# Experts of a decoder layer: ScalarE writes the high part of each Gelu result, VectorE only subtracts

## The chip, the cores and the metric

The kernel runs on one core of a Trainium2 chip. The metric is the device time of one execution in microseconds (us), from the first to the last instruction and what little lies around them. The time of the kernel before is the median of three runs. Everything else that is said of it comes from one further execution, which the hardware profiler recorded.

## The reference

One decoder layer in float32: self attention with a residual and a layer norm, cross attention to a context with a residual and a layer norm, and then a layer of eight experts, again with a residual and a layer norm. Only the experts are touched. Each token goes to the one of 8 experts with the highest logit; an expert takes at most 768 of the 4096 tokens (rows of 512 values).

```
buf = jnp.zeros((E, C, D), dtype=x.dtype).at[chosen_e, pos_c].add(x_flat * kept[:, None])
h = jax.nn.gelu(jnp.einsum('ecd,edf->ecf', buf, w1) + b1[:, None, :], approximate=False)
eo = jnp.einsum('ecf,efd->ecd', h, w2) + b2[:, None, :]
y = eo[chosen_e, pos_c] * (chosen_p * kept.astype(x.dtype))[:, None]
```

with E = 8 experts, C = 768 slots, D = 512 and F = 2048 hidden values.

## The kernel before, in words

Three stages follow each other: self attention (lines up to about 700), cross attention (to about 1570) and `experts` (from 1572). Only `experts` is changed. The trace has its first matmul at 2783.6 us.

**What is computed how.** TensorE multiplies in the rounded format fp32r. To keep float32's precision, every operand is held in two parts, a high part (the value rounded to fp32r) and a low part (the value minus its high part), and each product is three matmuls: high x high, high x low, low x high (`PARTS`). So weights, inputs and hidden values all go through two elementwise instructions: a rounding copy, and a subtraction that needs the copy.

**Tiling.** The experts run one after the other. An expert's hidden values are made in 16 steps of 128 values (four quads of four steps; `q` counts quads, `j` steps within one). In step `j` TensorE does `first_layer(j)`, 12 matmuls for each half of the slots into `h_bank[0]` and `h_bank[1]` (a half is 384 slots, `HALF`), and then `second_layer(j - 1)`, three matmuls of 512 columns for each tile of 128 slots, summed in `acc[t]` over the whole expert. How many tiles an expert works on is chosen at run time from its count of tokens (`VARIANTS`: 3, 4, 5 or 6). With 3 tiles the second half has no columns and gets no matmuls, but ScalarE and VectorE still process both halves.

**ScalarE's order in a step** (one loop over all 32 quads, lines 1720 to 1738): the high part of w1 for step `j + 1` (L1717), the high part of w2 for step `j` (L1732, which waits for a `second_layer`), then the Gelu of each half from PSUM into `h` (L1737), each after its half's matmuls. Each quad has two loads of an activation table, one ahead of the first copy (L1717) and one ahead of the first Gelu (L1737).

**VectorE's order in a step** (`quad`, from 1787): the low part of w1 for step `j + 1` (L1763), the low part of w2 (L1792), then for each half the high part of `h` (L1798, wait for `h_ready`) and its low part (L1800, wait for `hT_hi`, which counts L1798), then whatever is due of the work for other experts: in the steps `j = 0` and `j = 1` of quads 1 to 3 `split_x` (L1756, L1758), which takes 128 transposed slots of the next expert's input out of `h_bank[0]` in two instructions; and pieces of the previous expert's residual and norm (L1771, L1774, L1776, L1784).

**Who waits for it.** `second_layer(j)` waits for `hT_ready`, which counts L1800. `first_layer` of the steps 1 and 2 of quads 1 to 3 waits for `x_ready`, which counts L1758 (the transposes of L1839 and the next `first_layer` use the same `h_bank[0]`), so each `split_x` stands between two matmul groups. SyncE loads the next weights when `w1_ready` and `w2_ready` say that L1763 and L1792 are through. GpSimd loads the next expert's rows (L1676) and scatters the previous expert's (L1690).

Of the kernel before, what the change touches and what calls it, by code (L numbers as in the profile page):

```python
# [10 lines left out]
ACT = mybir.ActivationFunctionType  # L11
# [24 lines left out]
def wait_alone(engine, sem, value, waited):  # L36

    engine.wait_ge(sem, value)
    engine.sem_inc(waited, 1)
# [1530 lines left out]
def experts(nc, z, a):  # L1573
# [13 lines left out]
    HALF = CAP // 2  # L1587
# [12 lines left out]
    with ExitStack() as ctx:  # L1600
# [11 lines left out]
        h = s.sb("h", [P, 2, CAP])  # L1612
        hT = s.sb("hT", [P, 2, 2, CAP], F32R)
# [16 lines left out]
        h_mm, h_ready, hT_hi, hT_ready = s.sem("h_mm"), s.sem("h_ready"), s.sem("hT_hi"), s.sem("hT_ready")  # L1630
# [81 lines left out]
        @block.scalar  # L1712
        def _(act):
            def high_w1(hidden, j):

                act.wait_ge(h_mm, hidden + 2 * FREE)
                act.activation(w1[:, j % 2, 0, :, :], w1_in[:, j // 2, :, j % 2 * P:(j % 2 + 1) * P], ACT.Copy).then_inc(w1_hi, 1)  # L1717

            act.wait_ge(b1_ready, 1)
            act.wait_ge(w_in[0], 32)  # L1720
            high_w1(0, 0)
            with act.Fori(0, E * QUADS) as eq:
                n = act.snap(eq * 4)
                n2 = act.snap(eq * 8)
                for j in range(4):

                    if j % 2:
                        act.wait_ge(w_in[(j + 1) // 2 % 2], (eq + 1 + (j + 1) // 4) * 32)
                    high_w1(n2 + 2 * j, (j + 1) % 4)

                    act.wait_ge(o_mm, n + j - 1 + FREE)
                    act.activation(w2[:, j % 2, 0, :], w2_in[:, j // 2, j % 2, :], ACT.Copy).then_inc(w2_hi, 1)  # L1732
                    for half in range(2):
                        act.wait_ge(h_mm, n2 + 2 * j + half + 2 * FREE + 1)

                        act.wait_ge(hT_ready, n2 + 2 * j + half - 3 + 2 * FREE)
                        act.activation(h[:, j % 2, half * HALF:(half + 1) * HALF], h_bank[half][:, 0:HALF], ACT.Gelu,  # L1737
                                       bias=b1[:, bass.ds(n + j, 1)]).then_inc(h_ready, 1)

        @block.vector  # L1740
        def _(dve):

            for t in range(VARIANTS[0], TS):
                dve.memset(acc[t][:, :], 0.0).then_inc(acc0, 1)
            dve.sem_inc(hT_ready, 2 * FREE)
            dve.sem_inc(w1_ready, FREE)
            dve.sem_inc(w2_ready, FREE)
            dve.wait_ge(b1_mm, 1)
            dve.tensor_copy(b1[:, :], acc[0][:, 0:E * STEPS]).then_inc(b1_ready, 1)

            def split_x(e, t, buf, bank):

                cols = slice(t * P, (t + 1) * P)
                src = bank[:, :].rearrange("p (k q) -> p k q", k=KC)
                dve.wait_ge(x_mm, e * TS + t + 1)
                dve.tensor_scalar(xT[:, buf, 0, :, cols], src, 0.0, None, ALU.add).then_inc(x_hi, 1)  # L1756
                dve.wait_ge(x_hi, e * TS + t + 1)
                dve.tensor_tensor(xT[:, buf, 1, :, cols], src, xT[:, buf, 0, :, cols].bitcast(F32), ALU.subtract).then_inc(x_ready, 1)  # L1758

            def low_w1(n, j):  # L1760

                dve.wait_ge(w1_hi, n + 1)
                dve.tensor_tensor(w1[:, j % 2, 1, :, :], w1_in[:, j // 2, :, j % 2 * P:(j % 2 + 1) * P],  # L1763
                                  w1[:, j % 2, 0, :, :].bitcast(F32), ALU.subtract).then_inc(w1_ready, 1)

            def add_rows(e, t):


                dve.wait_ge(in_rows, (e + 1) * 16)
                dve.wait_ge(out_ready, e * TS + t + 1)  # L1770
                dve.scalar_tensor_tensor(out=out[:, t, :], in0=out[:, t, :], scalar=rows[:, t, C:C + 1],  # L1771
                                         in1=rows[:, t, 0:C], op0=ALU.mult, op1=ALU.add).then_inc(sum_ready, 1)
                dve.wait_ge(sum_ready, e * TS + t + 1)
                dve.bn_stats(stat[:, t, :], out[:, t, :]).then_inc(stat_ready, 1)  # L1774
                wait_alone(dve, stat_ready, e * TS + t + 1, waited)
                dve.bn_aggr(mv[:, t, :], stat[:, t, :]).then_inc(mv_ready, 1)  # L1776

            def add_eps(e):
                dve.wait_ge(mv_ready, (e + 1) * TS)
                dve.tensor_scalar(var_eps[:, :], mv[:, :, 1], EPS, None, ALU.add).then_inc(ve_ready, 1)  # L1780

            def scale_rows(e, t):
                dve.wait_ge(rstd_ready, e + 1)
                dve.tensor_scalar(out[:, t, :], out[:, t, :], mv[:, t, 0:1], rstd[:, t:t + 1], ALU.subtract, ALU.mult).then_inc(y_ready, 1)  # L1784

            def quad(e, q):
                par = e % 2
                n, n2 = (e * QUADS + q) * 4, (e * QUADS + q) * 8
                for j in range(4):
                    low_w1(n + j + 1, (j + 1) % 4)  # L1790
                    dve.wait_ge(w2_hi, n + j + 1)
                    dve.tensor_tensor(w2[:, j % 2, 1, :], w2_in[:, j // 2, j % 2, :], w2[:, j % 2, 0, :].bitcast(F32), ALU.subtract).then_inc(w2_ready, 1)  # L1792

                    dve.wait_ge(o_mm, n + j - 1 + FREE)
                    for half in range(2):
                        cols = slice(half * HALF, (half + 1) * HALF)
                        dve.wait_ge(h_ready, n2 + 2 * j + half + 1)
                        dve.tensor_copy(hT[:, j % 2, 0, cols], h[:, j % 2, cols]).then_inc(hT_hi, 1)  # L1798
                        dve.wait_ge(hT_hi, n2 + 2 * j + half + 1)
                        dve.tensor_tensor(hT[:, j % 2, 1, cols], h[:, j % 2, cols], hT[:, j % 2, 0, cols].bitcast(F32), ALU.subtract).then_inc(hT_ready, 1)  # L1800
                    if q > 0 and j < 2:
                        split_x(e + 1, 2 * q - 2 + j, 1 - par, h_bank[0])
                    if e > 0 and (q, j) in ADD_AT:
                        add_rows(e - 1, ADD_AT[q, j])
                    if e > 0 and (q, j) == EPS_AT:
                        add_eps(e - 1)
                    if e > 0 and (q, j) in SCALE_AT:
                        for t in SCALE_AT[q, j]:
                            scale_rows(e - 1, t)

            for t in range(TS):
                split_x(0, t, 0, h_bank[t % 2])
            low_w1(0, 0)
            for e in range(E):
                for q in range(QUADS):
                    quad(e, q)
                dve.wait_ge(in_b2, (e + 1) * 16)

                dve.wait_ge(scattered, e * TS * 16)
                dve.wait_ge(o_mm, (e + 1) * STEPS + FREE)  # L1820
                for t in range(TS):
                    dve.tensor_tensor(out[:, t, :], acc[t][:, :], b2[:, :], ALU.add).then_inc(out_ready, 1)  # L1822
            for t in range(TS):
                add_rows(E - 1, t)
            add_eps(E - 1)
            for t in range(TS):
                scale_rows(E - 1, t)
# [159 lines left out]
```

## Time and profile before

| | |
|---|---|
| median of 3 runs | 3785.6 us (3783.69 to 3785.71) |
| profiled execution | 3778.94 us |
| its span, first to last instruction | 3777.2 us |
| experts stage in the span | from 2783.6 us |
| PE, DVE, ACT, POOL busy over the span | 92%, 67%, 46%, 54% |
| mean granted TensorE clock | 0.955 |

PE is TensorE, DVE VectorE, ACT ScalarE, POOL GpSimd; PEld is TensorE's weight loading. A granted clock of 1.0 is 2.4 GHz, of 0.5 is 1.2 GHz. A group of instructions is named by its line in the kernel. The busy shares are means over three stages with different limits, so they say little on one edit in the last stage; that has to be read from the stage's own steps.

### The profile page before, as it was taken

How to read it: one execution, taken by the hardware profiler on the slowest of the kernel's cores; microseconds unless marked ns; L12 is line 12 of the kernel's file. 1: busy time of each engine (PE TensorE's matmuls, PEld its weight loads, DVE VectorE, ACT ScalarE, POOL GpSimd, SP SyncE). 2: the span in 40 equal slices, each digit the busy share in tenths (PEclk: the TensorE clock that was granted, in tenths of full speed). 3: DMA queues.
4: the chain of work that ended last, by engine and by line, in shares of the span. 5: the costliest groups of instructions: out<-in, count | busy, mean ns of one | idle time of the engine just before them, and what ended most of it. 6: DMA issues, size and time to landing. Idle time of an engine off the chain costs nothing. (4 is left out here: it accounts for less than half of the span.)

```text
span 3777.2 us, 51836 instructions
## 1 busy us (share of the span) xinstructions
PE 3470.1 (92%) x18133; PEld 2274.6 (60%) x18134; DVE 2519.5 (67%) x4522; ACT 1754.4 (46%) x3098; POOL 2045.9 (54%) x1031
## 2 busy tenths in 40 slices
PE   7999999999999999999999858899869889899985
PEld 5455455455454554554544336788758778788874
DVE  6777777777777777777777336788634755466566
ACT  2555555555555555555555533343323433343343
POOL 2789898888988898888898820011110100110112
PEclk9999999999999999999999878999879999999998
DMA  6321322313122223223110032222132422232332
GB/s 219 95 62 55 93 63 66 98 48 97 57 65 85 66 67 91 64 66 99 48 40 12 7 98 74 81 82 77 65 114 71 136 88 97 95 104 100 118 117 99
DMA packets 190735, 309.76 MB, mean 82 GB/s; under 512 B 25609, under 2 KB 72329, under 8 KB 190490
## 3 DMA queue, kind: packets, MB, share of 16 engines
q1 hardware_dynamic: 164330, 238.58, 20.3%
q0 software_dynamic: 15072, 45.89, 3.5%
q10 hardware_dynamic: 11088, 22.02, 1.7%
q8 instruction: 153, 2.51, 0.3%
q14 instruction: 92, 0.75, 0.1%
HBM read 197.23 MB, written 61.33 MB: 68 GB/s over the span
## 5 line engine op out<-in xcount | busy, mean ns | idle before, releaser
L463 DVE TENSOR_REDUCE sa_part_max<-sa_mx 128x1 f32<-128x512 f32 x2048 | 1281.9, 680 | 541.5 <-PE sa_mx L574 537.4
L426 ACT ACTIVATE sa_prob<-sa_sc 128x512 f32<-128x512 f32 x2048 | 1122.0, 595 | 822.5 <-PE sa_sc L620 780.8
L247 POOL TENSOR_TENSOR sa_quad_sum<-sa_quad_sum,sa_prob 128x1024 f32<-128x1024 f32 x512 | 1207.6, 2404 | 7.7 <-ACT sa_prob L426 7.7
L574 PE MATMUL sa_mx<-sa_k_stack,sa_q_stack 96*128 96x512 f32 x2048 | 967.2, 474 | 27.1 <-DVE sa_part_max L463 15.8
L620 PE MATMUL sa_sc<-sa_q_stack,sa_k_stack 98*128 98x512 f32 x2048 | 864.6, 424 | 8.2 <-ACT sa_prob L426 8.2
L247 POOL TENSOR_TENSOR sa_quad_sum<-sa_prob 128x1024 f32<-128x1024 f32 x256 | 616.1, 2429 | 256.1 <-ACT sa_prob L426 256.1
L574 PEld LDWEIGHTS sa_mx<-sa_k_stack,sa_q_stack 96*128 96x128 f32 x2048 | 389.4, 190 | 377.1 <-issue 205.0
L620 PEld LDWEIGHTS sa_sc<-sa_q_stack,sa_k_stack 98*128 98x128 f32 x2048 | 389.1, 190 | 318.8 <-ACT sa_prob L426 273.6
L1856 PE MATMUL ex_h<-ex_xT,ex_w 128*128 128x384 f32 (+2 forms) x2688 | 467.6, 330 | 81.9 <-issue 35.0
L1856 PEld LDWEIGHTS ex_h<-ex_xT,ex_w 128*128 128x128 f32 x2688 | 450.7, 196 | 106.4 <-issue 77.8
L589 PE MATMUL sa_pv<-sa_prob,sa_v 128*32 128x512 f32 x4096 | 501.9, 608 | 0.7 <-ACT sa_prob L426 0.7
L1867 PE MATMUL ex_acc<-ex_w,ex_hT 128*128 128x512 f32 x1728 | 433.3, 397 | 1.4 <-DVE ex_hT L1800 1.4
L1867 PEld LDWEIGHTS ex_acc<-ex_w,ex_hT 128*128 128x128 f32 x1728 | 318.5, 190 | 61.4 <-DVE ex_hT L1800 2.3
L1676 POOL DMA_DIRECT2D ex_xg<-rows x54 | 29.8, 559 | 549.7 <-PE ex_h L1839 549.4
L1798 DVE CAST ex_hT<-ex_h 128x384 fp32r<-128x384 f32 x256 | 92.3, 361 | 272.8 <-ACT ex_h L1737 272.8
L1737 ACT ACTIVATE ex_h<-ex_h,ex_b 128x384 f32<-128x384 f32 x256 | 143.9, 581 | 273.6 <-PE ex_h L1856 273.3
L589 PEld LDWEIGHTS sa_pv<-sa_prob,sa_v 128*32 128x32 f32 x4096 | 108.0, 110 | 245.0 <-issue 241.2
L927 POOL TENSOR_TENSOR ca_rstd<-ca_var_eps,ca_minus_half 128x8 f32<-128x8 f32 x16 | 26.5, 1656 | 393.7 <-DVE ca_var_eps L1010 393.7
L490 DVE RECIPROCAL sa_recip<-sa_dens 128x128 f32<-128x128 f32 x128 | 119.9, 941 | 77.4 <-ACT sa_dens L408 77.4
L1732 ACT ACTIVATE ex_w<-ex_w_in 128x512 fp32r<-128x512 f32 x128 | 80.7, 631 | 185.0 <-PE ex_acc L1867 184.3
L1800 DVE TENSOR_TENSOR ex_hT<-ex_h,ex_hT 128x384 fp32r<-128x384 f32 x256 | 143.0, 558 | 8.9
L1685 POOL TENSOR_TENSOR ex_rstd<-ex_var_eps,ex_minus_half 128x6 f32<-128x6 f32 x8 | 13.9, 1742 | 236.5 <-DVE ex_var_eps L1780 236.5
(201 smaller groups left out, 3397.1 us busy)
## 6 DMA issues: line engine op xcount, KB each, us to landing
ex_w_in<-in_L_ffn_w_dram SPq DMA_DIRECT2D x130, 512.0 KB, 4.3
sa_xT<-xT SPq DMA_DIRECT2D x57, 1024.0 KB, 5.1
sa_q_stack<-sa_hilo SPq DMA_DIRECT2D x372, 64.0 KB, 2.0
sa_k_stack<-sa_hilo SPq DMA_DIRECT2D x360, 64.0 KB, 2.0
ex_xg<-rows POOLq DMA_DIRECT2D x54, 256.0 KB, 3.2
rows<-sa_empty SPq DMA_DIRECT2D x48, 257.0 KB, 3.8
ex_rows<-rows POOLq DMA_DIRECT2D x8, 1542.0 KB, 7.5
sa_prob<-in_x_dram ACTq DMA_DIRECT2D x8, 1024.0 KB, 7.4
```

Of the source, the lines that this page charges most:

```text
L247: pool.tensor_tensor(quad_sum[:, i % 2, heads, :], so_far, prob[:, k, heads, :], ALU.add).then_inc(quad_ready, 1)
L426: act.activation(prob[:, kt % 4, j, :], sc[n % 2][:, :], ACT.Exp, scale=SCALE).then_inc(prob_ready, 1)
L463: dve.reduce_max(part_max[:, q, j, k:k + 1], mx[n % 3][:, :], AX_X).then_inc(max_read, 1)
L490: dve.reciprocal(recip[:, g % 2, cols], dens[:, cols]).then_inc(recip_ready, 1)
L574: pe.matmul(mx[n % 3][:, :], q_stack[0:QK, j, at:at + P], k_stack[0:QK, g // NQ % 2, j, k * BANK:(k + 1) * BANK], start=True, stop=True).t ...
L589: last = pe.matmul(pv[D * j:D * (j + 1), :], v[:, buf, kt, D * j:D * (j + 1)], prob[:, kt % 4, j, :], start=(kt == 0), stop=(kt == T - 1))
L620: pe.matmul(sc[n % 2][:, :], k_stack[0:AUG, g // NQ % 2, j, kt * P:(kt + 1) * P], q_stack[0:AUG, j, g % NQ * BANK:(g % NQ + 1) * BANK], st ...
L1737: act.activation(h[:, j % 2, half * HALF:(half + 1) * HALF], h_bank[half][:, 0:HALF], ACT.Gelu, bias=b1[:, bass.ds(n + j, 1)]).then_inc(h_ ...
L1798: dve.tensor_copy(hT[:, j % 2, 0, cols], h[:, j % 2, cols]).then_inc(hT_hi, 1)
L1800: dve.tensor_tensor(hT[:, j % 2, 1, cols], h[:, j % 2, cols], hT[:, j % 2, 0, cols].bitcast(F32), ALU.subtract).then_inc(hT_ready, 1)
L1856: last = pe.matmul(h_bank[half][:, 0:slots], w1[:, j % 2, pw, k, :], xT[:, buf, px, k, half * HALF:half * HALF + slots], start=(i == 0 and ...
L1867: last = pe.matmul(acc[t][:, :], hT[:, j % 2, ph, t * P:(t + 1) * P], w2[:, j % 2, pw, :], start=(start and i == 0), stop=(stop and i == 2))
```

## The change

The rounding copy of each half of `h` moves from VectorE to ScalarE. ScalarE issues both copies after both Gelus of the step, each behind a wait for its own Gelu. VectorE keeps the subtraction, whose wait for `hT_hi` is now a wait for ScalarE. Tiles, semaphores, counts and the number of instructions in all stay as they are.

```
@@ experts, scalar
                         act.activation(h[:, j % 2, half * HALF:(half + 1) * HALF], h_bank[half][:, 0:HALF], ACT.Gelu,
                                        bias=b1[:, bass.ds(n + j, 1)]).then_inc(h_ready, 1)
+                    for half in range(2):
+                        cols = slice(half * HALF, (half + 1) * HALF)
+                        act.wait_ge(h_ready, n2 + 2 * j + half + 1)
+                        act.activation(hT[:, j % 2, 0, cols], h[:, j % 2, cols], ACT.Copy).then_inc(hT_hi, 1)
@@ experts, vector, quad
                     dve.wait_ge(o_mm, n + j - 1 + FREE)
                     for half in range(2):
                         cols = slice(half * HALF, (half + 1) * HALF)
-                        dve.wait_ge(h_ready, n2 + 2 * j + half + 1)
-                        dve.tensor_copy(hT[:, j % 2, 0, cols], h[:, j % 2, cols]).then_inc(hT_hi, 1)
                         dve.wait_ge(hT_hi, n2 + 2 * j + half + 1)
                         dve.tensor_tensor(hT[:, j % 2, 1, cols], h[:, j % 2, cols], hT[:, j % 2, 0, cols].bitcast(F32), ALU.subtract).then_inc(hT_ready, 1)
```

## Rows read from the trace of the kernel before

**Rows 1.** Busy us by stretch (first line: columns): the stage, a 3-tile expert.

```profile
core 0: us, PE busy (x) PEld busy (x) DVE busy (x) ACT busy (x) POOL busy (x), PEclk, DMA share, GB/s
2784.00:3777.00 993.00, 878.06 (x4608) 785.26 (x4607) 579.58 (x1110) 373.18 (x573) 101.42 (x109) 0.95 0.30 101
...
2926.00:3026.00 100.00, 79.56 (x360) 68.66 (x360) 72.14 (x141) 45.67 (x72) 13.55 (x14) 0.91 0.40 134
```

**Rows 2.** Waits, 2784 to 3777 us: waiter <- releaser: us, times, longest.

```profile
PE ex_h L1856 <- DVE ex_xT L1758: 27.9, 30, 1.8
...
PE ex_acc L1867 <- DVE ex_hT L1800: 1.4, 2, 0.7
```

**Rows 3.** Groups by line and shape: busy us, mean ns | idle before.

```profile
L1737 ACT ACTIVATE ex_h<-ex_h,ex_b 128x384 f32<-128x384 f32 x256 | 143.9, 581 | 273.6 <-PE ex_h L1856 273.3
...
L1798 DVE CAST ex_hT<-ex_h 128x384 fp32r<-128x384 f32 x256 | 92.3, 361 | 272.8 <-ACT ex_h L1737 272.8
...
L1717 ACT ACT_TABLE_LOAD x32 | 41.1, 1283 | 0.6
L1737 ACT ACT_TABLE_LOAD x32 | 41.1, 1283 | 138.1 <-PE ex_h L1856 138.1
...
L1348 ACT ACTIVATE ca_qk<-ca_bank 128x154 fp32r<-128x154 f32 x16 | 4.8, 300 | 1.3 <-PE ca_bank L1540 0.9
...
L1259 ACT ACTIVATE ca_vw<-ca_product 128x512 fp32r<-128x512 f32 x8 | 4.4, 618 | 5.1 <-DMA vw<-ca_x1n 5.1
```

**Rows 4.** Timeline, 4-tile expert, step j = 0 with `split_x`: start, us, engine.

```profile
3449.53 1.06 ACT L1737 ACTIVATE ex_h<-ex_h,ex_b 128x384 f32<-128x384 f32 x2
3450.21 0.36 DVE L1798 CAST ex_hT<-ex_h 128x384 fp32r<-128x384 f32 x1 [2.88 <-ACT ex_h L1737]
...
3450.47 0.63 ACT L1717 ACTIVATE ex_w<-ex_w_in 128x512 fp32r<-128x512 f32 x1
...
3451.47 0.56 DVE L1800 TENSOR_TENSOR ex_hT<-ex_h,ex_hT 128x384 fp32r<-128x384 f32 x1
3451.95 0.68 DVE L1756 TENSOR_SCALAR ex_xT<-ex_h 128x512 fp32r<-128x512 f32 x1
...
3453.59 3.66 PE L1856 MATMUL ex_h<-ex_xT,ex_w 128*128 128x384 f32 x24 [0.99 <-DVE ex_xT L1758]
```

**Rows 5.** Timeline, the same expert, next step (j = 1).

```profile
3457.49 0.58 ACT L1737 ACTIVATE ex_h<-ex_h,ex_b 128x384 f32<-128x384 f32 x1 [0.71 <-PE ex_h L1856]
...
3459.16 0.69 DVE L1756 TENSOR_SCALAR ex_xT<-ex_h 128x512 fp32r<-128x512 f32 x1
```

**Rows 6.** Timeline, 5-tile expert, step j = 1, and the wait before it.

```profile
3332.86 3.78 PE L1856 MATMUL ex_h<-ex_xT,ex_w 128*128 128x384 f32 x24 [0.19 <-DVE ex_xT L1758]
...
3336.88 0.58 ACT L1737 ACTIVATE ex_h<-ex_h,ex_b 128x384 f32<-128x384 f32 x1 [0.85 <-PE ex_h L1856]
...
3338.51 0.69 DVE L1756 TENSOR_SCALAR ex_xT<-ex_h 128x512 fp32r<-128x512 f32 x1
...
3340.38 3.69 PE L1856 MATMUL ex_h<-ex_xT,ex_w 128*128 128x384 f32 x24
```

**Rows 7.** Timeline, 6-tile expert, step j = 1.

```profile
3196.08 0.69 DVE L1758 TENSOR_TENSOR ex_xT<-ex_h,ex_xT 128x512 fp32r<-128x512 f32 x1
...
3197.92 4.35 PE L1856 MATMUL ex_h<-ex_xT,ex_w 128*128 128x384 f32 x24
```

**Rows 8.** Timeline, 3-tile expert, from one quad to the next.

```profile
2944.86 1.05 ACT L1737 ACTIVATE ex_h<-ex_h,ex_b 128x384 f32<-128x384 f32 x2 [1.67 <-PE ex_h L1856]
...
2947.76 0.62 ACT L1732 ACTIVATE ex_w<-ex_w_in 128x512 fp32r<-128x512 f32 x1
...
2949.01 1.28 ACT L1737 ACT_TABLE_LOAD   x1 [0.63 <-PE ex_h L1856]
```

**Rows 9.** Timeline, PE alone, 3-tile expert: after two waits.

```profile
2954.37 4.21 PE L1856 MATMUL ex_h<-ex_xT,ex_w 128*128 128x384 f32 x12 [1.80 <-DVE ex_xT L1758]
...
3002.86 2.34 PE L1856 MATMUL ex_h<-ex_xT,ex_w 128*128 128x384 f32 x12 [1.80 <-DVE ex_xT L1758]
```

More of the change, by code:

```diff
@@ L1738, in _ @@
                                        bias=b1[:, bass.ds(n + j, 1)]).then_inc(h_ready, 1)
+                    for half in range(2):
+                        cols = slice(half * HALF, (half + 1) * HALF)
+                        act.wait_ge(h_ready, n2 + 2 * j + half + 1)
+                        act.activation(hT[:, j % 2, 0, cols], h[:, j % 2, cols], ACT.Copy).then_inc(hT_hi, 1)
         @block.vector
@@ L1796, in quad @@
                         cols = slice(half * HALF, (half + 1) * HALF)
-                        dve.wait_ge(h_ready, n2 + 2 * j + half + 1)
-                        dve.tensor_copy(hT[:, j % 2, 0, cols], h[:, j % 2, cols]).then_inc(hT_hi, 1)
                         dve.wait_ge(hT_hi, n2 + 2 * j + half + 1)
```

## The prediction

> **What bounds the kernel now.** I read the views in this order: busy time by stretch, then who waits for whom, then the timeline around each kind of wait, since the edit touches one stage only. In the experts stage TensorE is busy for 878 of 993 us, VectorE for 580 and ScalarE for 373 [rows 1]: TensorE sets the pace, and neither of the two engines that trade work is full. In a 3-tile expert PE is busy for only 80 of 100 us, and there VectorE is busy for 72 [rows 1]. The eight experts have 6, 3, 5, 6, 5, 4, 4 and 3 tiles (18, 9, 15 ... matmuls of L1867 a step).
>
> The instruction that moves, L1798, costs 256 x 361 ns = 92 us of VectorE [rows 3]. That is no gain by itself: VectorE idles for 272.8 us right before these casts, waiting for the Gelus [rows 3]. What counts is the chain from the Gelus to TensorE. TensorE waits for hidden values (L1800) for only 1.4 us in the whole stage, but for `split_x` (L1758) 30 times, 27.9 us [rows 2]. `split_x` stands in VectorE's queue right behind the second subtraction, so the edit acts through these 30 places. By expert they are: all 12 of the two 3-tile experts, all 12 of the two 4-tile experts, and the 6 with j = 0 in the two 5-tile experts; the 6-tile experts have none. That makes 18 with j = 0 and 12 with j = 1.
>
> **Price of the new instruction.** The trace has no ScalarE copy of 384 columns out of SBUF. Bounds: a copy of 512 columns takes 618 ns, one of 154 takes 300 ns (out of PSUM), and the Gelu of 384 takes 581 ns [rows 3]. The line between the two copies gives 300 + 230 x (618 - 300)/358 = 504 ns at 384 columns. The copies of this stage out of SBUF take 10 ns more than the 618 (L1717, 0.63 us [rows 4]), so I take 0.52 us, near that row, and keep 0.50 and, by the Gelu, 0.58 as ends. ScalarE starts the next instruction before the last has ended: the copy of L1717 starts 0.94 us after the first of two Gelus of 0.58 us each [rows 4], 0.47 us apiece, so an overlap of 0.1 us. A copy of 0.52 then occupies ScalarE for about 0.43 us. VectorE starts 0.10 us after a ScalarE result (Gelu from 3449.53, done after 0.58, cast at 3450.21) [rows 4].
>
> The VectorE cast takes 361 ns against 558 for the subtraction of the same size, so it is the cheaper engine for this copy. The Trainium skill (Perfetto Trace Analysis, Optimizing Scalar/DVE Operations) says that a copy for which VectorE has a fast mode is quicker there, and that moving it to ScalarE may pay where VectorE is saturated. By that rule the change loses; the trace agrees that VectorE is not saturated (580 of 993 us).
>
> The Trainium skill (VectorE: DVE Perf Modes, the section on the TRN2 errata) gives ScalarE's SBUF to SBUF cost as 224 cycles plus one per column at 1.2 GHz. That would be an estimate of 507 ns here and would put the sum below at about 7.4 us; no row shows that size.
>
> **(a) j = 0 steps, and 3-tile steps: both Gelus back to back.** Here the table load holds the Gelus until both halves are ready (or, with 3 tiles, both are ready at once), and they run as a pair. Count from the pair's start. Before: cast at 0.68, second subtraction at 1.94, `split_x` at 2.42 [rows 4]. After: the copies start at 0.95 and 1.38 and end at 1.47 and 1.90; the first subtraction starts at 1.57, the second 0.48 later (the distance from subtraction to next instruction in [rows 4]) at 2.05, `split_x` at 2.53. The cast that VectorE no longer does and the copies that ScalarE does in its place nearly cancel: +0.11 us. All 18 places with j = 0 wait already, so they pay it in full: 18 x 0.11 = 2.0 us. Of the six j = 1 places of the 3-tile experts, two follow a slow stretch of TensorE in which its own transposes (L1839) came last; the other four pay 4 x 0.11 = 0.4 us. The last `second_layer` of a 3-tile expert waits for the last subtraction: 2 x 0.11 = 0.2 us.
>
> **(b) j = 1 steps of 4-tile experts: the Gelus are apart.** Before, the first half's cast and subtraction were done while TensorE was still at the second half. After, both copies sit behind the second Gelu. It starts at 3457.49 [rows 5]; copies at 3457.97 and 3458.40, ending 3458.49 and 3458.92; subtractions at 3458.59 and 3459.07; `split_x` at 3459.55 in place of 3459.16 [rows 5], +0.39 us, all of it on TensorE's wait. 6 x 0.39 = 2.3 us.
>
> **(c) j = 1 steps of 5-tile experts: a new wait.** The second Gelu starts at 3336.88, `split_x` at 3338.51, and TensorE goes on at 3340.38 without waiting [rows 6]. By the same count `split_x` starts at 3338.94, +0.43. `split_x` takes 1.41 us and TensorE starts 0.23 after it (3451.95 to 3453.59 is 1.64) [rows 4], so TensorE starts at 3340.58 at the earliest, 0.20 late, and a group after a wait runs 3.78 us against 3.69 without [rows 6], since its first weights load in the open: 0.28 us in all. 6 x 0.28 = 1.7 us.
>
> **(d) 6-tile experts: nothing.** `split_x` ends at 3196.77, and TensorE takes it up at 3197.92 [rows 7]: 1.15 us of cover against 0.43 of delay. The 16 ordinary steps of any expert don't pay either: `second_layer(j)` starts a whole `first_layer` after the Gelus that it needs, over 3 us with 4 tiles or more, and 4.2 us from the Gelus' start with 3; the second subtraction ends at 2.61.
>
> **(e) What is queued behind the copies on ScalarE.** The copies of L1717 and L1732 and the table loads come 0.85 us later. In experts with 4 to 6 tiles ScalarE has that much idle time ahead of L1732 or the table load of L1737. With 3 tiles it hasn't at a quad's end: L1732 ends at 2948.38, and the table load of L1737 starts at 2949.01, when the matmuls are done [rows 8]. 0.85 later is 2949.23, so the load, the Gelus and `split_x` come 0.23 us later: 3 quads x 2 experts x 0.23 = 1.4 us. If L1732 were held further by a late weight, it would be more. VectorE's subtraction of L1763 starts at 2.53 and finds its high part finished at 2.44, 0.1 us of slack at no cost. SyncE's loads and GpSimd's queue shift by the same tenths and have nobody waiting on them.
>
> **(f) No more table loads.** There are 32 + 32 in 32 quads [rows 3], and L1732 runs behind Gelus in steps 1 to 3 of each quad without one. So a copy right behind a Gelu needs none. The Trainium skill (ScalarE: Activation LUTs, Table sets) has copy in every set; the trace agrees.
>
> Sum: 2.0 + 0.4 + 0.2 + 2.3 + 1.7 + 1.4 = 8.0 us. Against the profiled execution that is 3778.9 + 8.0 = 3786.9 us; the median of the runs is 6.7 us above that execution, so 3793.6 us. A copy of 0.50 us makes the sum about 7; one of 0.58 us (0.48 of occupancy) makes (a) 0.17, (b) 0.45, (c) 0.34 and (e) 0.33 apiece, 11 us in all.
>
> **Rivals.**
> *TensorE's clock.* In the 3-tile experts twelve waits of the same kind are followed by 12 matmuls in about 2.35 us at clock 1.0; after three of them it takes 4.21, 4.20 and 3.02 us, as at 2954.37 [rows 9], with a granted clock near 0.5. The edit makes the idle time before six of them 0.34 us longer. Each further slow group costs 1.86 us; with three to nine more it is 3793.6 + 6 to 17 = 3799 to 3811 us. For it: idle time stands before each fall. Against it: the same 1.80 us stands before a slow and a fast group alike. If instead the three slow groups fall away by the shift of phase, 4.4 us come back: 3789 us.
> *Hidden.* The copies start in Gelus' shadow and some waits end elsewhere (TensorE's transposes): (b) and (c) vanish if `split_x` is held by the transposes. Then +4 us, 3790 us. Against it: the computed starts lie 0.4 us after the transposes end.
> *Faster: VectorE is the late one.* If VectorE is still busy with other work when the pair of Gelus is done, the casts it sheds come off the chain. `split_x` starts 1.74 us after VectorE comes free before, 0.96 after; the edit wins as soon as VectorE comes free later than 0.79 us after the pair's start, and by 0.78 us beyond 1.57. In all 22 places of (a) that is -17 instead of +2.4: 3785.6 - 17 + 2.3 + 1.7 + 1.4 = 3774 us. Against it: the casts there start at 0.68 us, released by the Gelu, after an idle time [rows 4].
> *The edit doesn't do what it says*, for instance a table load per copy: over 3830 us. Point (f) speaks against it.
>
> **How the numbers follow.** Forecast 0.55 (3792 to 3797), more slow groups 0.19, fewer 0.10, hidden 0.11, faster 0.04, table loads 0.01. About 0.2%, 7.6 us here, is what a measurement of this kernel can tell from no change: above 3793.2 is slower, below 3778.0 faster. The forecast lies on that line; I give two thirds of its 0.55 to slower. Slower: 0.36 + 0.19 + 0.01 = 0.56; same: 0.19 + 0.10 + 0.11 = 0.40; faster 0.04. The range goes from the case of fewer slow groups or hidden copies, 3788, to the lower part of the clock case, 3803.
>
> **What the profile after would show.** Copies of 128x384 on ACT at 0.50 to 0.58 us; 64 table loads; in the pair steps `split_x` at 2.53 us from the Gelus' start, not 2.42; 36 waits of PE for L1758 and not 30, some 34 us in place of 27.9; the 6-tile experts unchanged in length. Wrong would be: a copy that waits for its Gelu's end and leaves ScalarE idle, casts' 92 us found again as a shorter stage, or a changed granted clock in the 3-tile experts.

## The result, and the profile after

The changed kernel takes 1.0018 of the time of the kernel before, 95% interval 1.0011 to 1.0025: medians 3791.3 us against 3785.65 us over 20 runs each. By the ratio that is 6.8 us more (4 to 9), where 8.0 were forecast; the two medians alone lie 5.7 us apart. 3791.3 us lies in the range. It is a real loss, since the interval excludes 1, but just under the 0.2% that the prediction took as its line, where it had put 0.56 above and 0.40 within.

The first of these lines, from the page of after, has each engine's busy time; behind it stand two groups (busy us, mean ns | idle before) and four waits of the experts stage (us, times, longest):

```profile
PE 3481.4 (92%) x18133; PEld 2282.3 (60%) x18134; DVE 2416.9 (64%) x4266; ACT 1856.3 (49%) x3354; POOL 2047.5 (54%) x1031
```

```profile
L1742 ACT ACTIVATE ex_hT<-ex_h 128x384 fp32r<-128x384 f32 x256 | 119.1, 517 | 0.0
...
L1737 ACT ACT_TABLE_LOAD x32 | 41.1, 1283 | 128.3 <-PE ex_h L1858 128.2
```

```profile
DVE ex_hT L1802 <- ACT ex_hT L1742: 419.6, 128, 12.8
...
PE ex_h L1858 <- DVE ex_xT L1762: 30.1, 31, 1.9
...
PE ex_h L1841 <- ACT ex_h L1737: 7.3, 6, 1.2
...
PE ex_acc L1869 <- DVE ex_hT L1802: 1.6, 2, 0.8
```

VectorE is 103 us lighter and the kernel is no faster: VectorE now idles 419.6 us ahead of its subtractions, where it idled 272.8 ahead of its casts [rows 3] and 8.9 ahead of its subtractions. ScalarE is 102 us heavier. Its new copy takes 517 ns (0.52 taken), and no table load was added. TensorE's waits for `split_x` (now L1760 and L1762) went from 27.9 to 30.1 us [rows 2].

The timeline of a 4-tile expert of after, first the step j = 0, then j = 1, to be laid beside [rows 4] and [rows 5]:

```profile
3457.28 1.05 ACT L1737 ACTIVATE ex_h<-ex_h,ex_b 128x384 f32<-128x384 f32 x2
...
3458.23 0.94 ACT L1742 ACTIVATE ex_hT<-ex_h 128x384 fp32r<-128x384 f32 x2
...
3458.85 1.03 DVE L1802 TENSOR_TENSOR ex_hT<-ex_h,ex_hT 128x384 fp32r<-128x384 f32 x2 [3.06 <-ACT ex_hT L1742]
...
3459.80 0.68 DVE L1760 TENSOR_SCALAR ex_xT<-ex_h 128x512 fp32r<-128x512 f32 x1
...
3461.44 3.65 PE L1858 MATMUL ex_h<-ex_xT,ex_w 128*128 128x384 f32 x24 [1.08 <-DVE ex_xT L1762]
...
3465.33 0.58 ACT L1737 ACTIVATE ex_h<-ex_h,ex_b 128x384 f32<-128x384 f32 x1 [0.71 <-PE ex_h L1858]
3465.81 0.93 ACT L1742 ACTIVATE ex_hT<-ex_h 128x384 fp32r<-128x384 f32 x2
...
3467.37 0.69 DVE L1760 TENSOR_SCALAR ex_xT<-ex_h 128x512 fp32r<-128x512 f32 x1
...
3469.01 3.63 PE L1858 MATMUL ex_h<-ex_xT,ex_w 128*128 128x384 f32 x24 [0.66 <-DVE ex_xT L1762]
```

In the pair step `split_x` starts 2.52 us after the Gelus (2.42 before), and TensorE's wait is 1.08 us (0.99 before). With the Gelus apart (j = 1) it starts 2.04 after the second Gelu (1.67 before), and the TensorE group behind it, at 3469.01, waits 0.66 us. In the kernel before it waited 0.29:

```profile
3460.81 3.64 PE L1856 MATMUL ex_h<-ex_xT,ex_w 128*128 128x384 f32 x24 [0.29 <-DVE ex_xT L1758]
```

In the 5-tile expert, step j = 1, the distance is 2.04 (1.63 in [rows 6]), and TensorE's weight loads, which followed each other before, now pause for 0.42 us:

```profile
3342.46 0.58 ACT L1737 ACTIVATE ex_h<-ex_h,ex_b 128x384 f32<-128x384 f32 x1 [0.85 <-PE ex_h L1858]
...
3344.50 0.68 DVE L1760 TENSOR_SCALAR ex_xT<-ex_h 128x512 fp32r<-128x512 f32 x1
...
3346.11 0.99 PEld L1858 LDWEIGHTS ex_h<-ex_xT,ex_w 128*128 128x128 f32 x6 [0.42 <-issue]
```

And the 3-tile expert at a quad's start, to be laid beside [rows 8]: the table load follows L1732 without a gap, and the transposes of L1841 wait 1.23 us for the first Gelu. The last row is the same wait in the kernel before (its L1839), 1.02 us.

```profile
2953.18 0.61 ACT L1732 ACTIVATE ex_w<-ex_w_in 128x512 fp32r<-128x512 f32 x1
...
2953.81 1.28 ACT L1737 ACT_TABLE_LOAD   x1
...
2956.02 0.65 PE L1841 MATMUL ex_h<-ex_ident,ex_xg 128*128 128x128 f32 x4 [1.23 <-ACT ex_h L1737]
```

```profile
2951.22 0.65 PE L1839 MATMUL ex_h<-ex_ident,ex_xg 128*128 128x128 f32 x4 [1.02 <-ACT ex_h L1737]
```

### The profile page after: what moved, and what is told of

It is laid out like the page before. It is cut to its first block and busy times, and to the rows that moved or that the text cites. A ratio compares the mean times of both kernels' runs of the same rounds, so it can differ in the third digit from the quotient of the medians.

```text
span 3790.8 us, 52092 instructions
## 1 busy us (share of the span) xinstructions
PE 3481.4 (92%) x18133; PEld 2282.3 (60%) x18134; DVE 2416.9 (64%) x4266; ACT 1856.3 (49%) x3354; POOL 2047.5 (54%) x1031
## 5 line engine op out<-in xcount | busy, mean ns | idle before, releaser
L574 PE MATMUL sa_mx<-sa_k_stack,sa_q_stack 96*128 96x512 f32 x2048 | 967.6, 474 | 27.5 <-DVE sa_part_max L463 15.9
L1802 DVE TENSOR_TENSOR ex_hT<-ex_h,ex_hT 128x384 fp32r<-128x384 f32 x256 | 131.5, 555 | 419.6 <-ACT ex_hT L1742 419.6
L1737 ACT ACTIVATE ex_h<-ex_h,ex_b 128x384 f32<-128x384 f32 x256 | 143.8, 581 | 271.0 <-PE ex_h L1858 270.6
L597 PE MATMUL sa_den<-sa_quad_sum,sa_ones 128*32 128x512 f32 x1024 | 135.4, 601 | 4.4 <-POOL sa_quad_sum L247 4.4
L1732 ACT ACTIVATE ex_w<-ex_w_in 128x512 fp32r<-128x512 f32 x128 | 80.3, 628 | 109.5 <-PE ex_acc L1869 109.4
```

Of the source, the lines that this page charges most:

```text
L574: pe.matmul(mx[n % 3][:, :], q_stack[0:QK, j, at:at + P], k_stack[0:QK, g // NQ % 2, j, k * BANK:(k + 1) * BANK], start=True, stop=True).t ...
L597: last = pe.matmul(den[D * j:D * (j + 1), :], ones[:, :], quad_sum[:, d % 2, j, :], start=(d % QUADS == 0), stop=(d % QUADS == QUADS - 1))
```

## The experiments

Theory A is the prediction's: the edit costs time only where it makes `split_x` later, or holds ScalarE's table load. Theory B came from the two traces: part of the cost is TensorE's clock in the 3-tile experts. Against both stand the rivals named in each expectation. Ratios are to the kernel before on the same chip. "Stage" is the time from the first expert's output additions (L1822 of the kernel before) to the last expert's, in the profiled run of each; it leaves out the first expert, and is 826.1 and 832.3 us in the two traces of the kernel before, 829 in the mean. A "slow group" is one of the six groups of 12 matmuls that stand behind the j = 0 waits of the two 3-tile experts, where it takes over 2.4 us in place of 2.35. The stage varies by several us between traces of one kernel. What hardly varies is the length of a quad without slow groups, from one `split_x` with j = 0 to the next: 27.5 us in the 4-tile experts of both traces of the kernel before, 29.24 with 5 tiles and 34.15 with 6.

**The changed kernel again.**

> The changed kernel again, so that the others stand beside it on one chip, and a second trace of it. Theory A (the copies lengthen the chain from the Gelus to split_x, by 0.11 us where the Gelus are a pair and by 0.4 us where they are apart, and the table load of the 3-tile experts comes 0.2 us later): about +7 us over the kernel before, with split_x 2.5 us from the pair's start. Theory B (part of the cost is TensorE's clock in the 3-tile experts): the number of slow matmul groups there is again six where the kernel before has three. If it differs from trace to trace, B is chance and no effect of the edit.

Ratio 1.0022 (1.0009 to 1.0036), stage 833.6 us (837.2 in the first trace of after). The waits of the 4-tile experts and the j = 0 waits of the 3-tile experts repeat to 0.01 us, the j = 0 waits of the 5-tile experts to 0.03. The quads are 27.9 us long with 4 tiles, 29.57 with 5 and 34.15 with 6, in both traces of the changed kernel. Slow groups: five of six, where B expected six again.

**The kernel before again.**

> The kernel before, unchanged, for a second trace of it and the spread of the comparison: ratio 1.000 within its interval. Theory B asks how many slow matmul groups the 3-tile experts have in it: three as in the first trace if the edit changed that, any number if it is chance.

Ratio 1.0004 (0.9993 to 1.0015). Four of the six groups are slow (3.84, 4.20, 3.79, 4.21 us), three in the first trace. So the number varies by itself, and two traces of each don't settle B; it is taken up again below.

**Each copy right behind its own Gelu.**

```
                         act.activation(h[:, j % 2, half * HALF:(half + 1) * HALF], h_bank[half][:, 0:HALF], ACT.Gelu,
                                        bias=b1[:, bass.ds(n + j, 1)]).then_inc(h_ready, 1)
-                    for half in range(2):
                         cols = slice(half * HALF, (half + 1) * HALF)
                         act.wait_ge(h_ready, n2 + 2 * j + half + 1)
                         act.activation(hT[:, j % 2, 0, cols], h[:, j % 2, cols], ACT.Copy).then_inc(hT_hi, 1)
```

> Each copy stands right behind its own Gelu (Gelu 0, copy 0, Gelu 1, copy 1), the rest as in the changed kernel. The copy now waits for the end of the Gelu just ahead, so ScalarE cannot overlap them. Theory A: in the pair steps copy 0 from 0.70 to 1.22 us, Gelu 1 from 1.13, copy 1 from 1.83 to 2.35, split_x at 2.93, that is 0.51 later than before the change in 22 places (11 us); the table load of the 3-tile experts 0.67 late in 6 places (4 us), the experts' ends 1 us; but in the j = 1 steps of the 4-tile experts, where the Gelus are apart, only 0.13 in place of 0.37. In all about +17 us over the kernel before. Rival (the cost follows ScalarE's work, wherever it stands): +7 us as for the changed kernel.

Ratio 1.0031 (1.0019 to 1.0042): +12 us (7 to 16), stage 839.6. Timeline, 4-tile expert, j = 0:

```profile
3457.04 0.58 ACT L1737 ACTIVATE ex_h<-ex_h,ex_b 128x384 f32<-128x384 f32 x1
3457.65 0.53 ACT L1741 ACTIVATE ex_hT<-ex_h 128x384 fp32r<-128x384 f32 x1
3458.08 0.57 ACT L1737 ACTIVATE ex_h<-ex_h,ex_b 128x384 f32<-128x384 f32 x1
...
3458.68 0.53 ACT L1741 ACTIVATE ex_hT<-ex_h 128x384 fp32r<-128x384 f32 x1
...
3459.71 0.68 DVE L1759 TENSOR_SCALAR ex_xT<-ex_h 128x512 fp32r<-128x512 f32 x1
```

The direction is A's, the size is not: a copy that needs the Gelu just ahead starts 0.03 us after its end (0.61 from its start), where 0.12 was assumed, so `split_x` comes at 2.67 us and not at 2.93. With what the trace shows, 22 x 0.25 = 5.5, the transposes of the 3-tile experts waiting 1.51 in place of 1.02, 6 x 0.49 = 2.9, and the ends 0.5 make 9 us. Slow groups, six of six here, add some 4 us to that (see theory B). The 4-tile j = 1 waits are back at 0.29 us, as A says for Gelus apart, while the j = 0 waits grew to 1.25: the cost sits where the order of the copies puts it. The time alone doesn't settle it, since the rival's +7 lies at the edge of the interval and the changed kernel beside it at +8; the next two experiments do.

**VectorE keeps half 0, ScalarE takes half 1.** `b1_ready`, which stands at 1 when the steps begin, counts ScalarE's copies.

```
+                    cols = slice(HALF, 2 * HALF)
+                    act.wait_ge(h_ready, n2 + 2 * j + 2)
+                    act.activation(hT[:, j % 2, 0, cols], h[:, j % 2, cols], ACT.Copy).then_inc(b1_ready, 1)
...
-                        dve.wait_ge(h_ready, n2 + 2 * j + half + 1)
-                        dve.tensor_copy(hT[:, j % 2, 0, cols], h[:, j % 2, cols]).then_inc(hT_hi, 1)
-                        dve.wait_ge(hT_hi, n2 + 2 * j + half + 1)
+                        if half == 0:
+                            dve.wait_ge(h_ready, n2 + 2 * j + 1)
+                            dve.tensor_copy(hT[:, j % 2, 0, cols], h[:, j % 2, cols]).then_inc(hT_hi, 1)
+                            dve.wait_ge(hT_hi, n + j + 1)
+                        else:
+                            dve.wait_ge(b1_ready, n + j + 2)
```

> VectorE keeps the rounding copy of half 0, ScalarE takes only that of half 1, behind both Gelus. Theory A: in the pair steps VectorE has half 0 done at 1.6 us, the copy of half 1 starts when Gelu 1 is done and issued, 1.16, and ends at 1.68, second subtraction at 1.78, split_x at 2.26, 0.16 earlier than in the kernel before in 22 places (-3.5 us); in the j = 1 steps of the 4- and 5-tile experts 0.13 to 0.17 late in 12 places (+1.3 us); the table load not late. In all -2.5 us against the kernel before. Rival (the cost follows ScalarE's work): half of the change's, +3.5 us.

Ratio 0.9980 (0.9968 to 0.9991): -8 us (-12 to -3), stage 817.0. The gain was forecast at only 2.5 us, outside the interval.

```profile
3449.63 1.05 ACT L1737 ACTIVATE ex_h<-ex_h,ex_b 128x384 f32<-128x384 f32 x2
...
3450.72 0.52 ACT L1741 ACTIVATE ex_hT<-ex_h 128x384 fp32r<-128x384 f32 x1
...
3451.75 0.68 DVE L1759 TENSOR_SCALAR ex_xT<-ex_h 128x512 fp32r<-128x512 f32 x1
...
3453.39 3.63 PE L1862 MATMUL ex_h<-ex_xT,ex_w 128*128 128x384 f32 x24 [0.69 <-DVE ex_xT L1761]
```

The two engines work side by side and `split_x` starts at 2.12 us, 0.30 earlier than in the kernel before (0.16 expected, again because the copy's wait was taken too long): 22 x 0.30 = 6.6 us. The j = 1 waits of the 4-tile experts stay at 0.29 us, where 0.13 to 0.17 more had been expected. Moving half of the same work gains where moving all of it loses, so ScalarE's load as such is not the price; the rival's +3.5 is outside the interval.

**Each copy twice.**

```
                         act.wait_ge(h_ready, n2 + 2 * j + half + 1)
+                        act.activation(spare[:, j % 2, half, :], h[:, j % 2, cols], ACT.Copy)
                         act.activation(hT[:, j % 2, 0, cols], h[:, j % 2, cols], ACT.Copy).then_inc(hT_hi, 1)
```

> The changed kernel with each copy of ScalarE issued twice, the first one into a spare tile that nobody reads. Theory A: 0.43 us more per copy on the chain, in the pair steps split_x at 3.34 us, 0.92 later than in the kernel before, 22 places (20 us), in the j = 1 steps of the 4-tile experts +1.20 (7 us) and of the 5-tile experts +1.1 (7 us), the table load of the 3-tile experts 1.1 us late in 6 places (6.5 us), the experts' ends 2 us: about +43 us over the kernel before, six times the cost of the single copies, since the first copy was paid for by the cast that VectorE sheds. Rival (cost in proportion to the copies): +14 us.

Ratio 1.0148 (1.0122 to 1.0174): +56 us (46 to 66) from five runs, whose median lies 49 us above; stage 875.7, +46.5.

```profile
3473.98 1.05 ACT L1738 ACTIVATE ex_h<-ex_h,ex_b 128x384 f32<-128x384 f32 x2
...
3477.19 0.68 DVE L1762 TENSOR_SCALAR ex_xT<-ex_h 128x512 fp32r<-128x512 f32 x1
...
3478.84 3.63 PE L1860 MATMUL ex_h<-ex_xT,ex_w 128*128 128x384 f32 x24 [1.79 <-DVE ex_xT L1764]
```

`split_x` at 3.21 us (3.34 expected), all 36 places with 3 to 5 tiles wait. The rival's +14 is far outside. Of the remainder over 43, some 3 us are in the 6-tile experts, whose quads are 0.55 us longer (34.7 us) and had been left out; the rest is looked at under theory B.

**`split_x` ahead of the work on h**, in the kernel before and in the changed kernel, and with the shared copy.

```
+                    if q > 0 and j < 2:
+                        split_x(e + 1, 2 * q - 2 + j, 1 - par, h_bank[0])
                     dve.wait_ge(o_mm, n + j - 1 + FREE)
                     for half in range(2):
...
-                    if q > 0 and j < 2:
-                        split_x(e + 1, 2 * q - 2 + j, 1 - par, h_bank[0])
```

> The kernel before, with split_x moved in VectorE's order of a step ahead of the casts and subtractions of h (same instructions, same count). Theory A (TensorE waits for split_x only because it is queued behind the work on h): split_x starts when TensorE's transposes are done, 1.6 to 1.7 us from the pair's start and not 2.42; the 3-tile experts gain 0.83 in ten places, the 4-tile ones 0.72 in six, the 5-tile ones 0.27 in six: -14 us against the kernel before. Rival (the wait for split_x only hides another one, for hidden values or weights): under -4 us.

> The changed kernel with the same move of split_x. With split_x ahead, the copies are no longer on its chain. Theory A: all that is left of the edit's cost is the late table load and the end of the 3-tile experts, 1.4 us, so -12.8 us against the kernel before, and 1 to 2 us above the kernel before with split_x first. Rival (the edit's cost lies elsewhere: ScalarE's occupancy, memory contention, clock): it stays 7 us above the kernel before with split_x first, at -7 us.

> The copy shared (half 0 on VectorE, half 1 on ScalarE) and split_x first. Theory A: the work on h has slack either way, so within 1 us of the kernel before with split_x first, at -14 us against the kernel before. Rival (a lighter VectorE still pays): 2 us or more below it.

The first two were run a second time, side by side:

> The kernel before with split_x first, again: 0.995 of the kernel before. Theory B: its 3-tile experts wait 1.0 us at j = 0, and one or two of six groups are slow.

> The changed kernel with split_x first, again, beside the kernel before with split_x first on the same chip, to narrow the difference of the two. Theory A: 1 to 2 us above the other (table load and end of the 3-tile experts), both about 20 us below the kernel before. A cost of the copies that doesn't go through split_x would make it 5 us or more.

| kernel, `split_x` first | ratio | 95% interval | stage us |
|---|---|---|---|
| before | 0.9948 | 0.9933 to 0.9964 | 809.8 |
| before, again | 0.9944 | 0.9931 to 0.9958 | 806.8 |
| changed | 0.9941 | 0.9923 to 0.9959 | 811.1 |
| changed, again | 0.9948 | 0.9934 to 0.9961 | 810.4 |
| copy shared | 0.9951 | 0.9935 to 0.9966 | 808.1 |

Timelines, 4-tile expert, j = 0; first the kernel before with `split_x` first, then the changed one:

```profile
3445.30 1.05 ACT L1737 ACTIVATE ex_h<-ex_h,ex_b 128x384 f32<-128x384 f32 x2
...
3446.38 0.60 PE L1839 MATMUL ex_h<-ex_ident,ex_xg 128*128 128x128 f32 x4
...
3447.01 0.69 DVE L1756 TENSOR_SCALAR ex_xT<-ex_h 128x512 fp32r<-128x512 f32 x1 [3.92 <-PE ex_h L1839]
...
3448.66 3.66 PE L1856 MATMUL ex_h<-ex_xT,ex_w 128*128 128x384 f32 x24 [0.29 <-DVE ex_xT L1758]
```

```profile
3437.66 1.05 ACT L1737 ACTIVATE ex_h<-ex_h,ex_b 128x384 f32<-128x384 f32 x2
...
3439.38 0.69 DVE L1760 TENSOR_SCALAR ex_xT<-ex_h 128x512 fp32r<-128x512 f32 x1 [3.20 <-PE ex_h L1841]
...
3441.03 3.66 PE L1858 MATMUL ex_h<-ex_xT,ex_w 128*128 128x384 f32 x24 [0.29 <-DVE ex_xT L1762]
```

In both, `split_x` now starts when TensorE's transposes release it, 1.71 and 1.72 us from the pair, and the wait is 0.29 us in place of 0.99 and 1.08. This is the test of the mechanism: with the work on `h` out of the chain to `split_x`, the same edit costs -0.6 us in the mean of its two pairs of ratios (0.99445 against 0.9946), not +6.8, and by the spread of these runs about 3 us either way. In the mean of the stages it costs +2.5 us, where 1.4 were expected. The shared copy ends no lower than the kernel before with the same order (0.9951 against 0.9948 beside it), so a lighter VectorE gains nothing by itself there. All five runs of it beat the kernel before by 0.5 to 0.6%, about 20 us, so the rival that the wait for `split_x` only hides another one (under -4 us) falls. 14 us were expected; 1 more is in the 5-tile experts, whose quads are 0.43 us shorter where 0.27 were expected, and the rest is discussed under B.

**The edit in parts: in all steps but j = 1, and in the steps j = 1 alone** (VectorE keeps its casts in the others). ScalarE's part of the first edit is shown; the second has `j == 1` in its place.

```
+                        if j != 1:
+                            act.wait_ge(h_ready, n2 + 2 * j + half + 1)
+                            act.activation(hT[:, j % 2, 0, cols], h[:, j % 2, cols], ACT.Copy).then_inc(b1_ready, 1)
```

> ScalarE does the copies in the steps j = 0, 2 and 3 of each quad, VectorE keeps its casts in the steps j = 1. Theory A: the waits for split_x with j = 1 go back to those of the kernel before (0.29 us in the 4-tile experts, none in the 5-tile ones), those with j = 0 stay 0.10 longer, and the table load of the 3-tile experts stays 0.2 us late; +3.6 us over the kernel before, and the sum of TensorE's waits for L1758 near 29.7 us. Theory B (TensorE's clock falls more often the longer it has waited): the 3-tile experts' j = 0 waits stay at 1.9 us, so five or six of their six groups are slow, as in both traces of the changed kernel; three or four were in both traces of the kernel before, at 1.8 us.

> The complement: ScalarE does the copies only in the steps j = 1. Theory A: the j = 1 waits of the 4-tile experts are 0.66 us and the 5-tile experts run 0.27 us longer at j = 1, those with j = 0 are as in the kernel before and the table load is not late; +4.4 us over the kernel before. Theory B: the 3-tile experts' j = 0 waits are 1.8 us and three or four of six groups are slow, not five or six.

All but j = 1: 1.0004 (0.9995 to 1.0014), +1.5 us (-2 to 5). j = 1 alone: 1.0012 (1.0003 to 1.0021), +4.5 us (1 to 8). The sum is 6, against 6.8 for the whole edit, and both intervals hold A's figures (3.6 and 4.4), though neither tells them sharply. The traces do, place by place. TensorE's waits in a 4-tile expert, steps j = 0 and j = 1, first without j = 1, then with j = 1 alone:

```profile
3461.22 3.67 PE L1865 MATMUL ex_h<-ex_xT,ex_w 128*128 128x384 f32 x24 [1.09 <-DVE ex_xT L1763]
3468.44 3.64 PE L1865 MATMUL ex_h<-ex_xT,ex_w 128*128 128x384 f32 x24 [0.29 <-DVE ex_xT L1763]
```

```profile
3464.12 3.64 PE L1865 MATMUL ex_h<-ex_xT,ex_w 128*128 128x384 f32 x24 [0.99 <-DVE ex_xT L1763]
3471.68 3.63 PE L1865 MATMUL ex_h<-ex_xT,ex_w 128*128 128x384 f32 x24 [0.66 <-DVE ex_xT L1763]
```

Each half of the edit moves its own wait and leaves the other where the kernel before has it. The wait for the first Gelu at a quad's start of a 3-tile expert is 1.23 us without j = 1 and 1.02 with j = 1 alone, so the late table load goes with the copies of the other steps, as (e) says. The quads say the same: with 4 tiles they are 27.6 us long without j = 1 and 27.84 with j = 1 alone (27.5 before, 27.9 in the changed kernel), with 5 tiles 29.33 and 29.48. The total of 28.2 us of waits for L1763 misses the 29.7 expected, since the 3-tile experts' j = 1 waits are 1.0 to 1.6 us behind a slow group and 1.8 behind a fast one, and all six groups were slow. B fares worse: six slow groups came without j = 1, as it says, but five with j = 1 alone, where it expected three or four, and none in the kernel before with `split_x` first again, where it expected one or two.

**Theory B over all traces.** The rows are of after, TensorE alone, one 3-tile expert: three waits of 1.90 us with j = 0, each with the group behind it, and the first of the waits with j = 1 between. Below them stands the stretch of the first group and one of the second, where the number ahead of the DMA columns is the granted clock: 0.50 (1.2 GHz) and 1.00 (2.4 GHz).

```profile
2959.26 4.20 PE L1858 MATMUL ex_h<-ex_xT,ex_w 128*128 128x384 f32 x12 [1.90 <-DVE ex_xT L1762]
2967.94 2.35 PE L1858 MATMUL ex_h<-ex_xT,ex_w 128*128 128x384 f32 x12 [0.99 <-DVE ex_xT L1762]
2984.51 3.06 PE L1858 MATMUL ex_h<-ex_xT,ex_w 128*128 128x384 f32 x12 [1.90 <-DVE ex_xT L1762]
...
3008.57 3.21 PE L1858 MATMUL ex_h<-ex_xT,ex_w 128*128 128x384 f32 x12 [1.90 <-DVE ex_xT L1762]
```

```profile
2959.00:2963.00 4.00, 3.74 (x12) 3.75 (x13) 2.74 (x6) 0.00 (x0) 0.00 (x0) 0.50 0.00 0
2968.00:2970.00 2.00, 2.00 (x12) 2.00 (x13) 1.82 (x5) 0.00 (x0) 0.00 (x0) 1.00 0.64 244
```

Counting the six j = 0 groups of the two 3-tile experts in every trace, slow being over 2.4 us, and their excess over 2.35 us:

| wait at j = 0, us | kernels | slow groups of 6 | excess, us |
|---|---|---|---|
| 1.0 | five traces with `split_x` first | 1, 0, 2, 2, 1 | 1.8 in the mean |
| 1.5 | copy shared | 2 | 3.1 |
| 1.8 | before, twice; j = 1 alone | 3, 4, 5 | 4.4, 6.6, 6.2 |
| 1.9 | changed, twice; all but j = 1 | 6, 5, 6 | 6.8, 6.2, 7.6 |
| 2.05 | each copy behind its Gelu | 6 | 10.0 |
| 2.6 | each copy twice | 6 | 11.1 |

The longer the wait at j = 0, the more groups are slow, in fourteen traces of kernels that lengthen it in different ways. So B holds as a trend over kernels, but the wait alone can't be the cause. The 84 groups behind the j = 1 waits of the same experts in these traces are all fast (2.38 us at most), and 18 of them stand behind 1.76 to 2.54 us. What differs is what TensorE did before: at j = 0 its transposes have just waited for the first Gelu as well, and that wait grows along with the other (1.02 us before, 1.23 in the changed kernel, 1.51 with each copy behind its Gelu, 2.05 with each copy twice). Among the five traces with a j = 0 wait of 1.0 us, it is 1.0 us in three, with 2 slow groups of 18, and 1.2 in two, with 4 of 12. Which of the two waits counts isn't shown.

B's share in the changed kernel is the difference of the rows 1.9 and 1.8: 6.9 - 5.7 = 1.1 us, no more than the spread among equal kernels, so that for this edit it isn't shown. The whole stage says no more: TensorE was busy at a granted clock of 0.50 for 44 and 59 us in the traces of the kernel before and for 65 and 52 in those of the changed one. It is larger elsewhere: it takes off about 4 us when `split_x` goes first (15 by places, 19 with it, 20 measured), adds 4 to the copies right behind their Gelus (9 by places, 13 with it, 12 measured), and adds 5 to the doubled copies, where also two 4-tile groups behind 1.8 us of wait take 5.2 us in place of 3.65.

## Why the prediction came out as it did

- *What bounds the kernel* was right: where the edit costs, it is the chain to TensorE through `split_x`, in experts with 3 to 5 tiles. Taking `split_x` off that chain takes the edit's cost away (-0.6 us, within about 3 either way).
- *Price of the copy*: 0.52 us taken, 517 ns measured; 0.94 us for two, as computed.
- *(a)*: +0.11 us predicted, 0.09 to 0.10 measured on the waits (0.99 to 1.08, 1.80 to 1.90, 0.19 to 0.28). 1.8 us in 18 places for 2.0.
- *(b)*: +0.39 predicted, +0.37 measured. 2.2 us for 2.3.
- *(c)*: TensorE's group starts 3.50 us after the second Gelu before [rows 6] and 3.65 after (weights at 3346.11), 0.15 late where 0.20 was worked out. With the 0.08 of the open weight load, 6 x 0.23 = 1.4 us for 1.7; the quads give 29.57 - 29.24 - 0.09 = 0.24 each.
- *(d)*: the 6-tile expert takes 136.9 us from one expert's output additions to the next before and 136.7 after (139.6 and 136.8 in the second traces), and its quads take 34.15 us in all four: nothing, as said. The ordinary steps, of which an expert has 10 and not 16, paid nothing either: TensorE's waits for hidden values are 1.6 us for 1.4.
- *(e)*: 0.23 predicted, 0.21 measured, 1.3 us for 1.4; shown by the edit in parts.
- *(f)*: 32 table loads at L1737 as before, none ahead of a copy.
- The terms as measured make 7.3 us, with 0.6 us of (a)'s other 3-tile places taken as predicted, against a forecast of 8.0 and a measured 6.8. One place adds 0.35: in the last j = 1 step of the first 5-tile expert with `split_x`, in both traces of the changed kernel, the first subtraction starts only at the end of the second copy, and why stays open. That the sum and the measured time agree within 1 us is better than the interval (4 to 9) can confirm. The last step, from sum to median, added 8.0 to the median of three runs of the kernel before; that median hardly moved with 20 runs.
- *Rivals*: of the clock, the trend was right, the size for this edit (6 to 17 us more, three to nine more slow groups) wrong: there were two more in the mean of two traces, and the excess is 1.1 us larger, within the spread. "Hidden" and "VectorE is the late one" are refuted: in the changed kernel `split_x` starts at least 0.4 us after the transposes end wherever there are 4 or 5 tiles, and in the kernel before 124 of the 128 casts of a first half stand behind idle time of VectorE.
- *The signs named beforehand*: 36 waits for L1762 and some 34 us were forecast, 31 and 30.1 us came. Of the six new ones in the 5-tile experts only one is listed, the place named above: in the other five only the weight load pauses (0.42 us, listed under "issue"), and the last matmul of the group ahead is recorded up to the moment when the next one starts, so that no idle time is listed. The j = 1 waits of the 3-tile experts shrank behind slow groups. So this sum was a poor witness; the single places were a good one. A changed clock in the 3-tile experts was named as a sign of being wrong. It came in the first pair of traces (0.91 before and 0.87 after in the first of them) and not in the second (0.88 and 0.92), so it says nothing either way.
- The line at 0.2% lay inside the forecast's own width, so the split between "slower" and "same" could not be argued from the profile, only the time.

## What to carry to other kernels

Moving an elementwise step from a busy engine to an idler one is worth what it takes off the chain that another engine waits for, and not the relief: here VectorE waited for the Gelus, and with 92 us of casts less it idled 138 us more ahead of this work. Moving both copies made that chain 0.10 us longer, moving one made it 0.30 us shorter. Ask what stands behind the moved step in the queue that it feeds: the cost and the larger gain (0.5%) both lay in `split_x`, which needed none of the work on `h` and stood behind it. As long as something waits behind the two halves, splitting the pair between two engines (0.998) beat giving both to either; with `split_x` first it made no difference that shows (0.994 to 0.995 each way).

## What the runs showed of the hardware

- A ScalarE copy that waits by semaphore for the Gelu right ahead of it starts 0.03 us after that one's end, at 0.61 us from its start, while behind a Gelu that it doesn't need it starts at 0.47: the wait costs 0.14 us in all. I had reckoned with 0.23.
- TensorE's granted clock in the short groups with j = 0 (12 matmuls, 2.35 us) had fallen to 0.50 more often the longer the wait ahead of them: at 1.0 us of wait in 6 of 30 groups, at 1.5 in 2 of 6, at 1.8 in 12 of 18, at 1.9 in 17 of 18, and from 2.05 in 12 of 12. A slow group costs up to 1.86 us, many times the 0.1 us by which its wait grew. The wait just ahead is not enough: behind j = 1 waits of 1.76 to 2.54 us, with no wait of the transposes before them, none of 18 groups was slow. What sets which of the groups behind equal waits is slow stays open.
